# First stage of a two-pass mixture-of-experts kernel: roots on ScalarE, four row buffers, scatters in step with the norms

## The reference

```python
h = layernorm(x)                        # x: 8 x 2048 x 256 fp32
x = x + 0.5 * ffn(h)                    # mixture of experts
x = x + attn(layernorm(x))              # a scan with softplus gates
x = x + 0.5 * ffn(layernorm(x))

def ffn(x):                             # T = 16384 tokens, E = 32 experts, C = 640
    logits = xt @ w_router
    top1 = argmax(softmax(logits)); gate = probs[top1]
    pos = cumsum(onehot(top1))[token, top1] - 1
    accepted = pos < C
    slot = where(accepted, top1 * C + pos, E * C)
    buf = zeros(E * C + 1, H).at[slot].set(xt)
    y = (silu(buf @ w_gate) * (buf @ w_up)) @ w_down        # per expert
    return xt + where(accepted, y[slot] * gate, 0)
```

## Time and profile before

| | |
|---|---|
| median of three runs | 1667.85 us |
| profiled execution | 1666.74 us, span 1664.9 us |
| PE busy | 1393.6 us (84%) |
| DVE busy | 1165.8 us (70%) |
| ACT busy | 1157.7 us (70%) |
| POOL busy | 825.0 us (50%) |
| scatters of rows (L337), both passes | 256, 257.0 us, 1004 ns each |
| DMA, whole span | 250.13 MB, 150 GB/s |

### The profile page before, as it was taken

One profiled execution on the slowest core, in us unless ns is written; L12 is line 12 of the kernel. 1 busy time (PEld: TensorE's weight loads), 2 busy tenths in 40 slices (PEclk: granted clock), 3 DMA queues, 4 the chain that ended last, 5 costly groups with the idle time before them and its releaser, 6 DMA issues. The chain is left out here.

```text
span 1664.9 us, 33221 instructions
## 1 busy us (share of the span) xinstructions
PE 1393.6 (84%) x10908; PEld 1305.4 (78%) x10920; DVE 1165.8 (70%) x3107; ACT 1157.7 (70%) x2418; POOL 825.0 (50%) x1109
## 2 busy tenths in 40 slices
PE   3445561699999999779999999999936999999997
PEld 2223330699999999769999999999826999999997
DVE  3435363477778777558788788788855777877875
ACT  5656771577777777458888878788745777777774
POOL 3176777144443434423437767767471444434343
PEclk8656555799999999979999999999967999999999
DMA  9996544566666766340213323311124444444541
GB/s 360 378 325 216 181 150 165 171 195 232 228 214 210 236 218 195 134 152 14 77 52 94 93 63 91 94 46 62 52 79 122 123 116 135 143 141 122 157 139 36
DMA packets 196858, 250.13 MB, mean 150 GB/s; under 512 B 24618, under 2 KB 181976, under 8 KB 192592
## 3 DMA queue, kind: packets, MB, share of 16 engines
q1 hardware_dynamic: 169040, 204.23, 37.9%
q0 software_dynamic: 27648, 43.78, 7.6%
HBM read 128.05 MB, written 152.17 MB: 168 GB/s over the span
## 5 line engine op out<-in xcount | busy, mean ns | idle before, releaser
L904 PE MATMUL ps<-xs,ws 128*128 128x320 f32 x3072 | 465.8, 311 | 4.0 <-DVE hf L862 3.6
L904 PEld LDWEIGHTS ps<-xs,ws 128*128 128x128 f32 x3072 | 455.4, 189 | 5.2 <-issue 5.2
L337 POOL DMA_INDIRECT slots<-xn,r x256 | 257.0, 1004 | 129.1 <-issue 107.2
L739 POOL DMA_INDIRECT x_rows<-ys,oidx x160 | 162.7, 1017 | 245.5 <-DVE ys L847 206.1
L739 POOL DMA_INDIRECT out<-ys,oidx x160 | 162.3, 1014 | 245.2 <-DVE ys L847 200.9
L904 PE MATMUL ps<-ws,hs 128*128 128x256 f32 x1920 | 261.4, 288 | 10.8 <-DVE ys L847 7.9
L904 PEld LDWEIGHTS ps<-ws,hs 128*128 128x128 f32 x1920 | 238.5, 190 | 24.1 <-issue 22.3
L862 DVE TENSOR_TENSOR hf<-ps,sg 128x320 f32<-128x320 f32 x256 | 125.8, 491 | 144.4 <-ACT sg L791 144.2
L404 PE MATMUL ps<-cf,xn 128*128 128x128 f32 x512 | 100.4, 332 | 132.0 <-ACT xn L359 131.4
L359 ACT ACTIVATE xn<-x,r 128x256 f32<-128x256 f32 x256 | 139.2, 595 | 85.2 <-DMA slots<-xn,r 46.3
L760 ACT CAST xs<-ps 128x512 fp32r<-128x512 f32 (+1 forms) x192 | 98.5, 513 | 135.3 <-PE ps L897 135.3
(11 more groups left out here) (119 smaller groups left out, 2521.4 us busy)
## 6 DMA issues: line engine op xcount, KB each, us to landing
slots<-zero SPq DMA_DIRECT2D x32, 1300.0 KB, 9.9
xg<-slots SPq DMA_DIRECT2D x64, 650.0 KB, 4.2
x<-in_x SPq DMA_DIRECT2D x32, 512.0 KB, 5.9
x_rows<-x SPq DMA_DIRECT2D x32, 512.0 KB, 3.9
wraw<-in_w_gate SPq DMA_DIRECT2D x64, 256.0 KB, 2.9
wraw<-in_w_up SPq DMA_DIRECT2D x64, 256.0 KB, 3.3
wraw<-in_w_down SPq DMA_DIRECT2D x64, 256.0 KB, 3.8
x<-x_rows SPq DMA_DIRECT2D x32, 512.0 KB, 5.2
```

The lines of the kernel that those rows point to most:

```text
L337: nc.gpsimd.indirect_dma_start(out=self.slots, out_offset=bass.IndirectOffsetOnAxis(ap=self.slot[:, t % XR, k:k + 1], axis=0), in_=self.xn ...
L739: nc.gpsimd.indirect_dma_start(out=rows, out_offset=bass.IndirectOffsetOnAxis(ap=OIDX[:, e % YR, k:k + 1], axis=0), in_=YS[:, e % YR, k, : ...
L904: ins = pe.matmul(dst, left(a, k), right(b, k), start=(n == 0), stop=(n == len(terms) - 1))
```

## The change

In `route()`:

- The roots move from POOL to ACT: Ln and Exp (`act_rstd`), three steps ahead of the norm, with DVE adding the constant and negating the mean (`dve_moments`) and making the factors (`dve_factors`) one step ahead. The table that holds Ln and Exp is loaded at the start.
- The statistics' lead grows from two units for the first group to six from unit 8 on.
- POOL has only the scatters left. All wait for the fills, and those of step S wait until S units are normalised. They begin 20 steps behind the batch instead of 15.
- Four row buffers for the normalised rows and the factors instead of three (`x` keeps three).
- The parts of the choice come at steps 15, 16, 18 and 19, the exp and the count at 17.
- The evacuation is two steps behind the turn instead of one, with three PSUM banks; raw products and logits come later, too.
- SP: the first loads come ahead of the constants, fills are mixed with loads 6 to 11, store 0 is issued ahead of the last six fills, and load q + 12 follows store q.

`attention()` calls the same class with three row buffers; there the waits on counts of earlier batches are one batch looser.

```diff
 BIG = 3 << 20
-XR = 3
...
                 self.xt = s([P, 2, HC, 2 * CH, P])
                 self.lt = s([P, 2, P])
                 self.d = s([P, TB, E])
                 self.cand = s([P, TB, E])
...
+                self.based = count(f"{tag}_based", 3 * NC + 1)
                 self.turned = count(f"{tag}_turned")
-                self.evac = count(f"{tag}_evac", 2)
+                self.evac = count(f"{tag}_evac", 3)
...
@@ -245,12 +245,12 @@
 
             def pool_rstd(self, pool, g):
                 lo, hi = self.groups[g]
-                t, r, n = lo // NC, lo // NC % XR, CH * (hi - lo)
+                t, r, n = lo // NC, lo // NC % RR, CH * (hi - lo)
                 k = slice(CH * lo % TB, CH * lo % TB + n)
                 if lo % NC == 0:
-                    pool.wait_ge(self.ready.sem, self.ready.at(min(t - 2, BATCH - 2)))
-                    pool.wait_ge(self.normed.sem, self.normed.at(NC * (t - 2)))
-                    pool.wait_ge(self.based.sem, self.based.at(NC * (t - 2)))
+                    pool.wait_ge(self.ready.sem, self.ready.at(min(t - 3, BATCH - 2)))
...
@@ -273,9 +273,10 @@
 
             def dve_moments(self, dve, g):
                 lo, hi = self.groups[g]
-                r, n = lo // NC % XR, CH * (hi - lo)
+                r, n = lo // NC % RR, CH * (hi - lo)
                 k = slice(CH * lo % TB, CH * lo % TB + n)
-                dve.wait_ge(self.rdone.sem, self.rdone.at(g - 1))
+                if self.own and g - 2 < self.own:
...
@@ -288,25 +289,28 @@
 
             def act_rstd(self, act, g):
                 lo, hi = self.groups[g]
...
-                    act.wait_ge(self.ready.sem, self.ready.at(t - 2))
+                    act.wait_ge(self.ready.sem, self.ready.at(min(t - 3, BATCH - 2)))
                 act.wait_ge(self.stats.sem, self.stats.at(g + 1))
+                if g - self.own >= 2:
+                    act.wait_ge(self.powered.sem, self.powered.at(g - self.own - 1))
                 apart(act)
-                act.activation(self.ln[:, 0:n], self.ve[:, r, k], ACT.Ln).then_inc(self.logged.sem, 1)
+                act.activation(self.ln[:, g % 2, 0:n], self.ve[:, r, k], ACT.Ln).then_inc(self.logged.sem, 1)
                 act.wait_ge(self.logged.sem, self.logged.at(g - self.own + 1))
-                act.activation(self.rb[:, r, k], self.ln[:, 0:n], ACT.Exp, scale=-0.5).then_inc(self.powered.sem, 1)
+                act.activation(self.rb[:, r, k], self.ln[:, g % 2, 0:n], ACT.Exp, scale=-0.5).then_inc(self.powered.sem, 1)
 
...
                 if lo % NC == 0:
-                    dve.wait_ge(self.normed.sem, self.normed.at(NC * (t - 2)))
-                    dve.wait_ge(self.based.sem, self.based.at(NC * (t - 2)))
-                dve.wait_ge(self.rdone.sem, self.rdone.at(g))
-                dve.wait_ge(self.scaled.sem, self.scaled.at(g))
+                    dve.wait_ge(self.normed.sem, self.normed.at(NC * (t - 3)))
+                    dve.wait_ge(self.based.sem, self.based.at(NC * (t - 3)))
+                if self.own:
+                    dve.wait_ge(self.rdone.sem, self.rdone.at(g))
...
@@ -335,13 +339,13 @@
                 apart(pool)
                 for k in tiles:
                     nc.gpsimd.indirect_dma_start(
-                        out=self.slots, out_offset=bass.IndirectOffsetOnAxis(ap=self.slot[:, t % XR, k:k + 1], axis=0),
-                        in_=self.xn[:, t % XR, k, :], in_offset=None, bounds_check=DROP - 1, oob_is_err=False,
-                    ).then_inc(self.scattered[t % XR], 16)
+                        out=self.slots, out_offset=bass.IndirectOffsetOnAxis(ap=self.slot[:, t % self.xr, k:k + 1], axis=0),
+                        in_=self.xn[:, t % self.xr, k, :], in_offset=None, bounds_check=DROP - 1, oob_is_err=False,
+                    ).then_inc(self.scattered[t % self.xr], 16)
 
             def all_scattered(self, sp):
-                for k in range(XR):
-                    sp.wait_ge(self.scattered[k], 16 * TB * len(range(k, BATCH, XR)))
+                for k in range(self.xr):
+                    sp.wait_ge(self.scattered[k], 16 * TB * len(range(k, BATCH, self.xr)))
...
@@ -350,14 +354,14 @@
 
             def act_norm(self, act, n):
                 t = n // NC
-                if n % NC == 0 and t >= XR:
-                    act.wait_ge(self.scattered[t % XR], 16 * TB * (t // XR))
+                if n % NC == 0 and t >= self.xr:
+                    act.wait_ge(self.scattered[t % self.xr], 16 * TB * (t // self.xr))
                 act.wait_ge(self.rdone.sem, self.rdone.at(self.group_of[n] + 1))
...
@@ -375,15 +379,16 @@
 
             def act_base(self, act, n):
                 t = n // NC
-                act.wait_ge(self.based.sem, self.based.at(n))
+                if self.own:
+                    act.wait_ge(self.based.sem, self.based.at(n))
                 act.wait_ge(self.normed.sem, self.normed.at(n + 1))
...
@@ -539,8 +544,12 @@
                 for t in range(BATCH):
                     w = 2 if t in (0, BATCH - 1) else 4
                     groups += [(NC * t + lo, NC * t + lo + w) for lo in range(0, NC, w)]
-                tail = Tail(st, "p1", (0, 1), (2, 3), 4, 6, 7, groups, stream, slots1)
-                LEAD, POST, SCATTER, BASE = 4, 11, 15, 3
+                tail = Tail(st, "p1", 4, 0, (0, 1, 5), (2, 3), 4, 6, 7, groups, stream, slots1)
+                POST, SCATTER, BASE = 15, 20, 3
+
+                PARTS = [(0, 1, 3, 4) if t < BATCH - 1 else (0, 1, 2, 3) for t, lo, hi in CHOICES]
+
+                lead = [min(6, 2 + lo // 2) for lo, hi in groups]
...
@@ -551,26 +560,35 @@
 
                 @block.sync
                 def _(sp):
+                    stream.load(sp, 0)
+                    stream.load(sp, 1)
                     sp.dma_start(CF[:], c_f32).then_inc(s_const, 16)
-                    for q in range(4):
-                        stream.load(sp, q)
+                    stream.load(sp, 2)
+                    stream.load(sp, 3)
                     sp.dma_start(CB[:], c_bf16).then_inc(s_const, 16)
                     sp.dma_start(TOK[:], c_u32).then_inc(s_const, 16)
                     sp.dma_start(WR[:], w_router.rearrange("(a p) e -> p a e", p=P)).then_inc(s_const, 16)
                     for k, w in enumerate((w_proj0, w_delta_t, w_r_t)):
                         sp.dma_start(WIN[:, 2 * k:2 * k + 2, :], w.rearrange("(a p) e -> p a e", p=P)).then_inc(s_w, 16)
                     sp.dma_start(DV[:], d_vec.to_broadcast([P, 1])).then_inc(s_w, 16)
-                    for q in range(4, 8):
+                    sp.wait_ge(zeroed, 1)
+                    stream.load(sp, 4)
+                    stream.load(sp, 5)
+                    nf = 0
+                    for q in range(6, 4 * XR):
+                        for n in range(nf, nf + 2 - q % 2):
+                            fill(sp, 0, slots1, n)
+                        nf += 2 - q % 2
                         stream.load(sp, q)
-                    sp.wait_ge(zeroed, 1)
-                    for n in range(NFILL):
+                    fill(sp, 0, slots1, nf)
+                    stream.store(sp, 0, tail.based)
+                    for n in range(nf + 1, NFILL):
                         fill(sp, 0, slots1, n)
-                        if n % 2 == 1 and n // 2 < 4:
-                            stream.load(sp, 8 + n // 2)
                     for q in range(NQ4):
-                        stream.store(sp, q, tail.based)
-                        if q >= 1 and q - 1 + 4 * XR < NQ4:
-                            stream.load(sp, q - 1 + 4 * XR)
+                        if q:
+                            stream.store(sp, q, tail.based)
+                        if q + 4 * XR < NQ4:
+                            stream.load(sp, q + 4 * XR)
@@ -581,15 +599,13 @@
 
                 @block.gpsimd
                 def _(pool):
-                    tail.pool_setup(pool)
                     nc.gpsimd.memset(ZERO[:], 0.0).then_inc(zeroed, 1)
                     pool.wait_ge(s_const, 64)
-                    for S in range(-LEAD, NU + SCATTER):
-                        for g, (lo, hi) in enumerate(groups):
-                            if lo - LEAD == S:
-                                tail.pool_rstd(pool, g)
-                        if S == SCATTER:
-                            pool.wait_ge(filled[0], 16 * NFILL)
+                    pool.wait_ge(filled[0], 16 * NFILL)
+                    for S in range(SCATTER, NU + SCATTER):
+
+                        if S <= NU:
+                            pool.wait_ge(tail.normed.sem, tail.normed.at(S))
                         for u in range(NC):
                             for c in choices(S, SCATTER + u):
                                 if 2 * u < CHOICES[c][2] - CHOICES[c][1]:
@@ -599,36 +615,44 @@
                 def _(act):
                     tail.act_setup(act)
                     tail.based.grant(act)
-                    for S in range(NU + 14):
```

(42 more changed lines are left out.)

55 lines of the change are left out of this document (30 added, 25 removed).

## The result

The kernel after the change takes 1646.4 us as a median of four runs (1645.8 to 1647.4), beside 1667.8 for the kernel before (four runs, 1665.0 to 1667.9). The ratio is 0.988, with a 95% interval of 0.9868 to 0.9892. That is 21.4 us less; the forecast was 29.2 less. The profiled execution took 1646.49 (span 1644.7), where 1637.5 was forecast, 9.0 us too low. The time lies in the stated range, and the stage is bound as forecast up to a point: it ends 40 scatters behind the last norm. What makes the last norm late is not what the forecast's sum had, but what one of its rivals named: SP's round of load and store.

What follows compares the result with a forecast made beforehand. POOL's queue bounds the first stage; afterwards last norm (214.7) + 0.3 + 40 scatters (51.1) = 266.1 against 295.3, 29.2 us less: 1666.74 - 29.2 = 1637.5, as a median 1638.6. Range 1625 to 1657, chance 0.80.

Steps and rivals of the forecast that it cites:

- What bounds the kernel: First stage: from 78 us on POOL's queue of 128 scatters and 13 groups' roots sets the stage's end.
- The count of gaps on POOL: POOL, first to last scatter: of 217.3 us, 9.6 are waiting, the rest scatters (163.5) and roots (44.2).
- The start: First stage, waiting for load 13: norm 20 at 92.6 instead of 83.5, first scatter at 92.3 instead of 78.0.
- The tail: End of the first stage on POOL: 40 scatters of 1.28 us behind norm 63, 51.1 us.
- The new operations: ACT in the first stage: Ln and Exp take 0.35 us a group, 4.2 us for twelve groups.
- SP's queue: First stage's rounds of store, landing, load: 5.6 us for two units where ACT needs 5.7; nothing added.
- reserve: SP's loads in the first stage: some 10 us to spare at the first groups.
- SP's round becomes the bound: Rival, first stage's 18 loads: 6.3 us a round costs 13 us, 1651; chance 0.17 for 6.1 to 7.2 us.
- The slower rival: SP's round at backlog length: no gain left at 7.7 us, 1686 at the longest landing; chance 0.06, no change 0.03.
- DVE's step at 8t + 20: First stage: ACT waits for DVE's factors 1.4 us in each of four batches, 5.6 us in all.
- The last landing: From the first stage's last scatter to the second stage's first read: stays as it is.

Runs made afterwards that it cites:

- The shorter lead: The kernel after with the statistics' lead capped at five units instead of six: 1643.8 us, 0.9855 of the kernel before.
- the lag: The kernel after with SP's load of quarter q + 11, not q + 12, behind store q, so one turn behind its store: 1633.6 us.
- the best kernel: The kernel after with loads one turn behind their store, lead at most five, roots one step ahead of the norm instead of three: 1625.5 us.

## Why the prediction was right, and where it was off

**What bounds the kernel: right.** With the roots gone from POOL, and nothing else, the stage ends 30.4 us earlier (295.3 to 264.9). With only a fourth row buffer ACT's wait just changes its name. The count of gaps on POOL (9.6 us) held as a bound. After the change it is "end of the last norm plus 40 scatters", as the prediction has it.

**The start: right.** Load 13 was there at 84.4 (86.2), norm 20 at 90.4 (92.6), the first scatter at 91.3 (92.3), all within the bounds of 87 to 97 and for the reason given. But the text counts "POOL's start loses 14 us" as if it were part of the price. The shorter lead gives the start back and, in the kernel after, moves the end by 0.3 us. POOL's start had no weight as long as the end is "end of the last norm plus 40 scatters", which the next part of the text says itself.

**The tail: right in size, and not weighed.** Norm 63 ends at 221.3 and the last scatter at 273.1: 51.8, summed with 51.1 + 0.3. But the text takes the 40 scatters as given. Beside the roots alone, with 30 scatters and 37.5 us behind the last norm, 14.3 of the 51.8 are a price of the change. **The new operations: right.** Roots 0.35.

**SP's queue: the mis-sized term.** The sentence "I take 4.9 plus two issues of 0.46, one in part beside the landing: 5.6 us" put a store behind a load at 4.9. It took 6.0, the round 6.46. Rows for it were at hand: with nothing ahead of it a store had 3.1 and the load behind one 5.4, and I set the store in the round below that load, though it now lies behind a load itself. How much of the 6.0 comes from that load and how much from the scatters beside it, no run separates. "A tie, with some 10 us in reserve at the first groups; I add nothing" then turned 0.86 us a round into nothing, where 18 rounds make 15.5. About half of it, 7.6, went into the reserve, and 7.9 into ACT: its waits from norm 20 on were 13.5 us (the 11.0 shown and 2.5 of small ones) instead of 5.6. The other terms give 1.3 back (2.2 at the start, less 0.9 that I can't place), so the last norm is late by 6.6. The same page and section of the Trainium skill as in the prediction ("DMA: Bandwidth & Descriptors", "Anatomy of one DMA") would give 4.4 for that store, an estimate that holds no other queue's traffic and rests on a fit for DMAs that GpSimd issues, where these are SP's; the 6.0 measured decides. With a store that has nothing ahead of it (3.1) the trace agrees with it, and with this one not.

**The rival "SP's round becomes the bound"** stood at 6.3 us and 1651; it came with 6.46 and 1646.4. The forecast's own range held the time, but in this part it is the rival's mechanism that the trace shows: the lag alone brings 12.9 us. That the time still fell in the range owes as much to the reserve as to the sum. Its price was too high: 18 rounds by 0.7 made 13 us, and at 6.46 by the same rule 15.5, where 9.0 were missing in all, because it left the reserve out. The slower rival (rounds of 7.7) did not come: one store took 8.4 us, but the median was 6.0.

**DVE's step at 8t + 20: right mechanism, wrong cause of its size.** I had 1.4 us from DVE's own work. With the lag it is 0.8 to 0.9. The rest of the 3.0 to 4.3 us is SP's loads, late.

**The last landing: missed.** I had "The landing and the next stages stay as they are". From the last scatter's end to the second stage's first read it became 4.3 us instead of 2.8.

**SP's queue, missed once more in an experiment.** For SP's rule alone on the kernel before I had at most 3 us, since POOL was the bound. It cost 7.9. The landing of a scatter was on the path, and it grows with what else is in flight.

What stays open: 0.9 us of ACT's 131; what the kernel would take with the lag, the roots on ACT and the choice as early as before (no run has it, and the tail's 14.3 us are read from kernels that differ in more than the steps of choice and scatter); and what a shorter count on PE would do to POOL's waits for a batch's slots.

## What to carry to other kernels

A queue that issues, waits for the landing, and issues again is a stage of its own: its round is the landing time, and it has to be set against the bound engine's time for the same data, with the landing taken among the traffic that there will be. Here they were 5.6 and 5.7 us on paper and 6.46 and 5.7 in the trace; a tie on paper deserves a price for each round. Waiting for the transfer before the last instead of the last gave 12.9 us here, for one line. Count also what lies behind the bound engine's last step: here the scatters begin five steps later, and ten more of them lie behind the last norm, 14 us. And test the parts of a change alone: here one part gave 31 us, and the whole gave 21.

## What the runs showed of the hardware

**With the lag SP's transfers take longer each and bring more.** In the best kernel the median load landed in 6.0 us beside 4.7, the median store in 7.3 beside 6.0 (80 to 190 us), and the engines moved 352 GB/s beside 241 in 100 to 120 us, at a share of 1.04 beside 0.78. Its last load was issued at 152.0 instead of 196.2. With the lag alone the load's median was 5.7 and the store's 6.8 up to 120 us; later, when SP had caught up, 4.1.

**A scatter's landing doubles beside SP's traffic**: 2.6 us from its start to the norm that waits for it when SP was idle, 5.3 to 6.5 with SP's loads and stores of 512 KB in flight, at three batches each. The spacing of scatters that follow each other without a wait stayed at 1.28 us in every kernel, at DMA shares from 0.5 to 1.05.

**The wait for all scatters takes longer with four row buffers than with three.** From the end of the last scatter to the second stage's read are 2.8 to 2.9 us in all three kernels with three row buffers and 4.2 to 4.3 in all ten with four. It is not the landing: the last scatter landed 2.6 us after its start with three buffers and 2.7 with four (the two kernels with roots on ACT and the old steps). SP waits for one semaphore per buffer, and that is the only difference here that I know of; what the 1.4 us are made of, no run shows.
